# A graph network, expert mixture and attention kernel: four tables of node sums instead of two, and a sort that is numbered inside the edge stage

## The reference

```python
e = _mlp2(edge_feat, We1, be1, We2, be2)              # relu(e @ We1 + be1) @ We2 + be2
msg = jax.nn.relu(node_feat[src] + e)                 # 40000 x 256
out_h = jax.ops.segment_sum(msg, dst, num_segments=N_NODES)
out = _mlp2((1.0 + eps[0]) * node_feat + out_h, Wn1, bn1, Wn2, bn2)
```

## Time and profile before

| what | value |
|---|---|
| median of three runs | 2723.11 us (2719.55 to 2726.37) |
| the profiled execution, its time on the device | 2718.02 us |
| its span in the profile | 2716.3 us |
| granted TensorE clock, mean over the span | 0.867 of full speed |
| busy: PE, DVE, POOL, ACT | 2088.1, 1647.1, 1394.8, 1007.2 us |
| costliest group: POOL L632, additions to the tables | 316, 551.3 us |
| POOL L623, gathers of node rows | 316, 327.3 us |

### The profile page before, as it was taken

The page is one execution under the profiler, slowest core; times in us unless marked ns, Lnnn a source line. Parts: engine busy times, 40 slices in busy tenths (PEclk is TensorE's granted clock), DMA queues, the critical chain, the costliest instruction groups (busy, mean ns, idle before and its releaser), DMA issues. The chain is left out here.

```text
span 2716.3 us, 46328 instructions
## 1 busy us (share of the span) xinstructions
PE 2088.1 (77%) x13095; PEld 1804.4 (66%) x13096; DVE 1647.1 (61%) x4774; ACT 1007.2 (37%) x1931; POOL 1394.8 (51%) x1131
## 2 busy tenths in 40 slices
PE   2599999999999999955629999990466666662778
PEld 2588888888888888855628888880444444441776
DVE  5477786666666666648464444445655555557774
ACT  1254445545445554432205555550222222221321
POOL 1387887877777877760001111105377777771000
PEclk9799999999999999977759999995777767765888
DMA  6466656666666666642116777762233333342001
GB/s 165 134 131 131 133 120 130 134 132 135 135 128 125 133 130 133 129 86 70 39 41 229 244 243 242 239 220 81 76 92 93 90 89 91 90 84 28 22 10 38
DMA packets 185998, 325.71 MB, mean 120 GB/s; under 512 B 27528, under 2 KB 109037, under 8 KB 185192
## 3 DMA queue, kind: packets, MB, share of 16 engines
q0 software_dynamic: 82080, 141.73, 25.8%
q1 hardware_dynamic: 102962, 181.83, 21.8%
q10 hardware_dynamic: 900, 1.50, 0.2%
HBM read 260.65 MB, written 64.30 MB: 120 GB/s over the span
## 5 line engine op out<-in xcount | busy, mean ns | idle before, releaser
L632 POOL DMA_INDIRECT edge_sums<-edge_agg,edge_slot x316 | 551.3, 1745 | 172.5 <-issue 78.8
L1750 POOL DMA_INDIRECT att_got<-head_table,att_idx x352 | 401.8, 1141 | 125.1 <-issue 107.0
L623 POOL DMA_INDIRECT edge_nf<-node_table,edge_node_idx x316 | 327.3, 1036 | 152.0 <-issue 89.0
L751 ACT ACTIVATE edge_whole<-edge_h_ps,edge_b 128x512 f32<-128x512 f32 x316 | 215.8, 683 | 482.2 <-PE edge_h_ps L468 478.4
L466 PE MATMUL edge_e_ps<-edge_w_high,edge_hid_low 128*128 128x256 f32 x1264 | 357.3, 283 | 0.1
L467 PE MATMUL edge_e_ps<-edge_w_low,edge_hid_high 128*128 128x256 f32 x1264 | 356.9, 282 | 0.0
L468 PE MATMUL edge_e_ps<-edge_w_high,edge_hid_high 128*128 128x256 f32 x1264 | 356.2, 282 | 0.0
L1780 PE MATMUL att_s_ps<-att_w,att_hot 128*125 128x258 f32 x704 | 277.0, 562 | 3.2 <-issue 1.8
L466 PE MATMUL edge_h_ps<-edge_eat_high,edge_w_low 128*128 128x512 f32 x632 | 248.9, 394 | 23.6 <-DVE edge_eat_low L811 23.6
L1361 POOL DMA_INDIRECT moe_rows<-node_table,moe_idx x54 | 51.9, 961 | 396.8 <-DVE moe_idx L1473 396.4
L825 DVE TENSOR_TENSOR edge_pre<-edge_e_ps,edge_nf 128x1024 f32<-128x1024 f32 x79 | 96.8, 1225 | 256.2 <-DMA edge_nf<-node_table,edge_node_idx 208.9
(11 more groups left out here) (344 smaller groups left out, 4424.4 us busy)
## 6 DMA issues: line engine op xcount, KB each, us to landing
moe_w<-in_L_ffn_w_dram SPq DMA_DIRECT2D x162, 512.0 KB, 4.7
edge_ea<-in_edge_attr_dram SPq DMA_DIRECT2D x77, 448.0 KB, 5.1
edge_dst_row<-dst_rows SPq DMA_DIRECT2D x79, 256.0 KB, 4.5
routed<-moe_out SPq DMA_DIRECT2D x54, 128.0 KB, 6.3
att_got<-head_table,att_idx POOLq DMA_INDIRECT x352, 2.8
edge_nf<-node_table,edge_node_idx POOLq DMA_INDIRECT x316
edge_sums<-edge_agg,edge_slot POOLq DMA_INDIRECT x316, 4.8
edge_ea<-in_edge_attr_dram SPq DMA_DIRECT2D x77, 64.0 KB, 5.3
```

Of the source, the lines that this page charges most:

```text
L623: pool.indirect_dma_start(nf[u][:, j, :], None, m.node_table[:, :], bass.IndirectOffsetOnAxis(ap=node_idx[u][:, j:j + 1], axis=0)).then_in ...
L632: pool.indirect_dma_start(m.sums[k][:, :], bass.IndirectOffsetOnAxis(ap=slot[u][:, j:j + 1], axis=0), agg[u][:, j, :], None, compute_op=AL ...
L751: act.activation(whole[c][:], h_ps[:, c % 2, 0:N], ACT.Relu, bias=b1[:, c:c + 1]).then_inc(hid_whole, 1)
L1750: pool.indirect_dma_start(got[v][:, j, :], None, m.head_table[:, :], bass.IndirectOffsetOnAxis(ap=idx[v][:, j:j + 1], axis=0)).then_inc(la ...
```

## The change

- `SUMS` becomes 4: each block of a group has its own table. POOL's additions to a table wait for those of the group before, `g * 16`. The tables that begin as zeros are three, and their DMAs (L606) stand right behind the weights, as soon as x has landed.
- PE's turn becomes `hidden(g)`, transposes, `edges_out(g)`, `gather_same(g-1)`.
- ACT makes all four high parts of the hidden layer, and the message's high part after them; DVE makes none. DVE's `one_group` begins with hidden low parts 0 and 1; then come `add_nodes`, low parts 2 and 3 and `message_low`.
- The sort is numbered in the edge stage: after group 23 PE computes the totals into the PSUM of the hidden layer, DVE takes the offsets and then numbers one bucket after each of groups 24 to 43 (`number_bucket`). The node stage no longer has `number`.
- The node stage loads four tables into SBUF, two of them in the space of `y` and `spare`; the weights go through ACT's queue. For each step POOL adds the tables 2 and 3, DVE 0 and 1, and then both.

The core of the diff:

```diff
-SUMS = 2
+SUMS = 4
@@ def edge_messages: SP
+                sp.wait_ge(zeros_ready, 1)
+                sp.wait_ge(m.x_landed, 32)
+                for k in range(1, SUMS):
+                    sp.dma_start(m.sums[k][0:N_NODES, :].rearrange("(p t) d -> p t d", t=TILES),
+                                 zeros[0:LANES, :].unsqueeze(1).to_broadcast([LANES, TILES, DIM])).then_inc(sums_begun, 16)
                 sp.wait_ge(rows_made, 1)
...
-                sp.wait_ge(zeros_ready, 1)
                 for k in range(SUMS):
                     sp.dma_start(m.sums[k][N_NODES:N_NODES + P, :], zeros[:]).then_inc(sums_begun, 16)
-                for k in range(1, SUMS):
-                    sp.dma_start(m.sums[k][0:N_NODES, :].rearrange("(p t) d -> p t d", t=TILES),
-                                 zeros[0:LANES, :].unsqueeze(1).to_broadcast([LANES, TILES, DIM])).then_inc(sums_begun, 16)
@@ POOL
-                def add_sums(g, u, n, first=False):
-                    for k in range(SUMS):
-                        j = n * SUMS + k
-                        if not (first and n == 0):
-                            pool.wait_ge(sum_landed[k], g * (16 * G // SUMS) + 16 * n)
+                def add_sums(g, u, tables, first=False):
+                    for k in tables:
+                        if not first:
+                            pool.wait_ge(sum_landed[k], g * 16)
...
@@ PE
-                    for u in range(2):
-                        hidden(g + u)
...
-                        transposes(1 - u, g * 16 + (32 + 32 * u))
-                        gather_same(g + (u - 1), 1 - u)
-                        edges_out(g + u)
+                        for u in range(2):
+                            hidden(g + u)
...
+                            transposes(1 - u, g * 16 + (32 + 32 * u))
+                            edges_out(g + u)
+                            gather_same(g + (u - 1), 1 - u)
...
+                turns(2, numbered)
+                pe.wait_ge(hid_whole, numbered * KH)
+                by_src.order.totals(pe, h_ps)
+                pe.wait_ge(by_src.order.offsets_ready, 1)
+                turns(numbered, tail)
@@ ACT
                 for c in range(KH):
                     hidden_relu(g, c)
-                    if c == 1 and first != 1:
-                        message_high(g - 1)
-                    if c % 2 == 0:
-                        even_high(g, c)
+                    hidden_high(g, c)
+                if first != 1:
+                    message_high(g - 1)
@@ DVE
+                for g in range(2 + TILES, numbered):
+                    one_group(g, g % 2)
+                by_src.order.offsets(dve, h_ps)
+                for g in range(numbered, numbered + TILES):
+                    one_group(g, g % 2)
+                    by_src.order.number_bucket(dve, g - numbered)
+                by_src.order.write_out(dve)
@@ class BucketSort
+    def number_bucket(self, dve, b):
...
+        one = slot[:] if b == 0 else self.part_i[:].bitcast(F32)
...
+        chain.link(nc.vector.scalar_tensor_tensor(one, self.seen[:, b, :], self.off[:, b:b + 1], self.mask[:, b, :], ALU.add, ALU.mult))
+        if b == 0:
+            chain.link(nc.vector.tensor_scalar(tile_f[:], units, last, None, ALU.is_ge))
+        else:
+            nc.vector.tensor_tensor(slot[:], slot[:], one, ALU.add)
+            chain.link(nc.vector.scalar_tensor_tensor(tile_f[:], units, last, tile_f[:], ALU.is_ge, ALU.add))
@@ def node_mlp
-        sums = [sb(f"sums{k}", [LANES, TILES, DIM]) for k in range(SUMS)]
+        sums = [m.y, m.spare] + [sb(f"sums{k}", [LANES, TILES, DIM]) for k in range(2, SUMS)]
...
+            @block.gpsimd
...
+                def add_late(n, u):
+                    nc.gpsimd.tensor_tensor(sums[2][:, tiles, :], sums[2][:, tiles, :], sums[3][:, tiles, :], ALU.add).then_inc(late_added, 1)
...
-                    nc.vector.tensor_tensor(z[u][:], sums[0][:, tiles, :], sums[1][:, tiles, :], ALU.add).then_inc(z_ready, 1)
+                    nc.vector.tensor_tensor(sums[0][:, tiles, :], sums[0][:, tiles, :], sums[1][:, tiles, :], ALU.add).then_inc(early_added, 1)
+                    dve.wait_ge(early_added, n + 1)
+                    dve.wait_ge(late_added, n + 1)
+                    nc.vector.tensor_tensor(z[u][:], sums[0][:, tiles, :], sums[2][:, tiles, :], ALU.add).then_inc(z_ready, 1)
...
-                by_src.order.number(dve)
```

More of the change, by code:

```diff
@@ L238, in __init__ @@
         self.tile_f = sb("tile_f", [1, self.units])
[L239 to L243, removed]
         if self.by_bucket:
-            self.numbers = ctx.enter_context(self.nc.sbuf_tensor(self.name + "_numbers", [LANES, self.buckets // 2, self.cols], F32))
-            self.part = ctx.enter_context(self.nc.sbuf_tensor(self.name + "_part", [LANES, self.cols], F32))
+            self.offsets_ready = sem(name + "_offsets_ready")
+        else:
+            self.sums = ctx.enter_context(nc.psum_tensor(name + "_sums", [P, 2, 512], F32))
     def count(self, dve):
@@ L275, in number @@
[L275 to L278, removed]
+        nc.tensor.matmul(sums[0:LANES, 0, 0:buckets], m.before[0:LANES, 0:LANES], self.mine[:], start=True, stop=True)
@@ new lines, in number @@
+    def number(self, dve):
+        nc, chain, units, buckets = self.nc, self.m.steps, self.units, self.buckets
+        mask, seen, last, off, slot = self.mask, self.seen, self.last, self.off, self.slot
+        self.offsets(dve, self.sums)
+        for b in range(buckets):
+            last_slots = nc.vector.scalar_tensor_tensor(seen[:, b, :], seen[:, b, :], off[:, b:b + 1], mask[:, b, :], ALU.add, ALU.mult)
+        chain.link(last_slots)
+        chain.link(nc.vector.tensor_reduce(slot[:], seen.rearrange("p b c -> p c b"), AX_X, ALU.add))
+        chain.link(nc.vector.tensor_tensor(
+            self.past, self.m.count[0:1, 0:units].unsqueeze(2).to_broadcast([1, units, buckets]),
+            last[0:1, :].unsqueeze(1).to_broadcast([1, units, buckets]), ALU.is_ge))
+        chain.link(nc.vector.tensor_reduce(self.tile_f[:], self.past, AX_X, ALU.add))
+        self.write_out(dve)
@@ L305, in number, with write_out @@
+    def write_out(self, dve):
+        nc, chain, out, slot, slot_i, part_i = self.nc, self.m.steps, self.out, self.slot, self.slot_i, self.part_i
         chain.link(nc.vector.tensor_copy(slot_i[:], slot[:]))
@@ L325, in _ @@
             def _(pe):
-                order.totals(pe)
+                order.totals(pe, order.sums)
             @block.vector
@@ L515, in edge_messages @@
     tail = (groups - 3) // 2 * 2
-    assert late % 2 == 0 and late <= tail
+    numbered = 2 + TILES + 2
+    assert late % 2 == 0 and late <= tail and SUMS == G
     with ExitStack() as ctx:
@@ L1043, in two @@
             return [sb(f"{n}{u}", shape, dt) for u in range(2)]
-        by_src.order.work(ctx)
         w1 = sb("w1", [P, KD, HID])
```

102 lines of the change are left out of this document (48 added, 54 removed).

## The result

The changed kernel takes 2778.1 us (2776.5 to 2785.8, 4 runs), the kernel before 2722.4 beside it: ratio 1.0209, 95% interval [1.0186, 1.0232], 56 us slower. The forecast was 2707 (2680 to 2738). The profiled spans are 2777.2 and 2716.3 us, 60.9 apart.

A forecast was written before the change was run, and what follows sets the result against it. POOL, never resting at 14.08 us a group, was taken to bound the loop. Terms: -47 (loop) + 8 + 3 (sort) + 15 (start) + 3.5 (node stage) + 1.5 (tail) = -16 us, giving 2707 us, range 2680 to 2738.

The forecast's parts named there:

- The loop: Edge loop: a group falls from 14.06 to 13.45 us, saving 47 us over 77 groups.
- A third loop binds these: Edge loop: later agg delays POOL's additions and so find_slots; with little room for gathers, 0.25 us a group added.
- POOL's own need: Edge loop: POOL needs 14.08 - 0.84 = 13.24 us a group without table waits, taken as 13.1.
- PE's own need: Edge loop: PE alone needs 12.88 us a group plus 0.3 for its new order, 13.2.
- The slot wait: Rival, edge loop: waits for slots replace table waits, T = 13.8 us a group, 2734 us in all; chance 0.22.
- The zeros are nearly free: Rival, start: SP queues all three tables and goes on, +3 instead of +15 us, 2695 in all; chance 0.15.
- the loads run faster: Rival, node stage: 11.3 MB at 300 GB/s take 38 us, 8 less, 2699 in all; chance 0.13.
- The sort: Edge loop: counting and numbering buckets cost 8 us, PE's stop at group 24 another 3 us.
- The start: Start: SP hangs behind three writes of zeros, node table leaves near 87.5 instead of 48.16 us; +15 us.
- The node stage: Node stage: numbering goes, but loads take 45.6 us, combine(2) is 4 us late and added sums cost 1.5; +3.5 us.

The follow-up runs named there:

- Gathers first: Changed kernel with POOL issuing all four gathers for group g+2 before it waits for agg(g), then the four additions: 2704.2 us, ratio 0.9932.
- the old turns: Changed kernel with the turns of PE, ACT and DVE as before, four tables and the sort in the loop kept: 2726.6 us, ratio 1.0012.
- fastest kernel: Changed kernel with POOL's four gathers ahead of its wait for agg and each table of zeros written by two DMAs: 2666.6 us, ratio 0.9825.
- the four buffers: Changed kernel with four slot buffers instead of two, written without waiting for the additions of the group before: 2761.6 us, ratio 1.0151.
- the edit to 112 + 13 partitions: Changed kernel with each table of zeros written by two DMAs, of 112 and 13 partitions, instead of one of 125: 2742.8 us, ratio 1.0079.
- the kernel with DVE's additions: Changed kernel with the node stage's sum of table 2 and table 3 on DVE instead of POOL: 2777.9 us, ratio 1.0227.
- the new turns alone: Kernel before with only the new turns of PE, ACT and DVE; two tables, zeros and sort as before: 2739.5 us, ratio 1.0049.

## Why the prediction was wrong

**The loop is the step that failed**, in the part "A third loop binds these". It gave 13.45 us a group, with 0.25 for a late landing of the additions and for the gathers, "landed about 4 us into the turn whose `add_nodes` comes at 5". The groups measured 14.39 us before the sort's part and 14.26 behind it, and the loop as a whole came out 69 us longer than forecast (+32.7 against -47 + 11), of the 77 us by which the profiled execution missed its 2702. The engines and the order of the loop were right, its closing was not: it was followed to `find_slots` and to the next low part, and the gathers were taken to have a microsecond to spare, when `add_nodes` waits for them in 44 of 61 groups. The lap above goes through the gathers and not through the slots: `agg`, 13.3 us of POOL's eight DMAs, a landing of 4.7, `add_nodes`, `edges_out`, `agg`, 28.6 for two groups, or 14.3 a group. With the new turns `agg` stands 6 us later, behind `edges_out`, and the gathers, though they do not need `agg`, stand behind it on POOL. Gathers first takes them out of the lap and gives 1.0 us a group back (0.2 of it by shorter issues); the old turns take `edges_out` out of it and give 0.7 back.

**POOL's own need was a term mis-sized.** "14.08 - 0.84 = 13.24", then 13.1, subtracted whole waits. But 0.30 us pass before every indirect DMA, a wait's row holds that gap too, and it stays when the wait goes. In the traces POOL needs its busy time plus 8 x 0.30: before 11.1 + 2.4 = 13.5, fastest kernel 11.0 + 2.4 = 13.4. With four tables and the gathers between the additions it is 13.6 to 13.7 (busy 11.24 in the old turns, 11.27 in the changed kernel). So even with waits at zero and no lap the forecast of 13.45 could not have been met. In the old turns four tables, with the sort in the loop, bring 14.05 to 13.77, a quarter of a microsecond; the full 0.84 was never there. The Trainium skill (Perfetto Trace Analysis, Identifying the Most-Contended Engine) judges GpSimd by its occupancy; here that was 79% for an engine that had nothing to give but 0.6 us a group, so the gaps belong to the sum.

**PE's own need was mis-sized too**, at 12.88 + 0.3 = 13.2. Before, 42 of the 76 groups take 12.88 us; with the new turns none takes less than 13.40. PE waits for the low parts of the hidden layer, as the forecast said, but for 0.26 us a group in the gathers-first kernel; the other quarter of a microsecond is not accounted for.

**The rivals.** "The slot wait" had the right sign (2734, T = 13.8), and DVE's waits for slots did grow to 244 us. Yet its mechanism carries 16 us of time, as the four buffers show, the largest part around groups 22 to 24. "The zeros are nearly free" and "the loads run faster" are refuted, by +17.9 us at the start and by the 49.8 us of the loads.

**The sort** was put at 8 + 3 us, and groups 22 to 44 took 14.91 us against 14.39 ahead of them, 11 us in all. That the sums agree is luck. The 19 groups 25 to 43, each with a bucket numbered behind it, took 14.32 us, those behind group 44 took 14.26: the numbering cost 1 us, and counting (14.39 in groups 2 to 22) under 3, against 4 each. Groups 23 and 24, at the totals and offsets, took 18.7 and 15.5, together 5.6 more than two groups of 14.3, against the forecast's 3. And group 22 took 21.8, for a reason that is not the sort's: it holds DVE's addition of `bn2` to x, which the kernel before has as well (14.9 us there), behind a slot wait of 5.1 us, and with POOL held by it:
```profile
419.42 0.16 DVE L864 TENSOR_TENSOR edge_slot<-edge_moves,edge_dst 128x4 int32<-128x4 f32 x1 [5.13 <-DMA edge_sums<-edge_agg,edge_slot]
...
420.79 5.48 DVE L934 TENSOR_TENSOR x<-x,row_a 125x5120 f32<-125x5120 f32 x1
...
421.72 5.44 POOL L632 DMA_INDIRECT edge_nf<-node_table,edge_node_idx  x1 [0.31 <-issue]
```
In the gathers-first kernel groups 22 to 24 take 17.8, 14.8 and 13.5 us, and those that number take 13.40 like all others. Nor is the sort what made the kernel slower: with it in the old turns the mean group is 13.77.

**The start** came as argued: SP hung for three writes at 0.34 of the DMA engines, 121 GB/s, the node table left at 85.04 (87.5 forecast), +17.9 against +15. The Trainium skill (DMA: Bandwidth & Descriptors, Why a DMA increments its semaphore by 16 and not by 1) has the outer size decide how many engines a DMA uses. With the forecast only the window stood for it; the edit to 112 + 13 partitions is the test, and the 70 us of hung issues before the node table became 36.

**The node stage** was +10.2 against +3.5. The order of events was right (weights, then a wait for the second part of the tables). Two terms were short: the loads took 49.8 us and not 45.6, as the 11.3 MB came at 227 GB/s and not at 247, and the stage behind them ran 1.9 us longer, not 0.5 shorter. Of that at most 1.2 us can be POOL's additions, by the kernel with DVE's additions, whose node stage is no shorter as a whole.

What stays open: the new turns cost 14 us with two tables and 52 with four. Part of it is that four tables gain 21 us in the old turns (14.05 to 13.77 a group, with the sort in the loop) and 4.5 at most in the new, where the lap of 14.3 binds either way. The other 20 us or so are not accounted for, and no profile of the new turns alone near its median is there to place them. The two comparisons also differ in the sort, which stands in the loop in both kernels of the 52 us and in neither of the 14.

## What to carry to other kernels

An engine whose busy time and ordinary gaps fill the window is full, whatever its busy share says; of a wait that will go, subtract only what exceeds the gap. When a wait on one queue goes, look for the loop through the instructions that stand behind another wait on that queue without needing it: moving the gathers ahead of it turned a change that lost 2.1% into one that gains 0.7. The two need each other: without the early gathers four tables gained next to nothing in the loop of the new turns, and with two tables the early gathers brought the mean group from 14.54 only to 14.32, with four from 14.48 to 13.48. And a copy is priced by how its outer size divides over the DMA engines before it is multiplied by three.

## What the runs showed of the hardware

- DVE and POOL slow each other on additions with both inputs in SBUF: on POOL one of 125x512 took 1.26 us alone and 1.70 to 1.74 beside DVE's, and DVE's took 1.78 and 1.64 beside POOL's, 0.69 alone. The Trainium skill (SBUF — State Buffer, Who interferes with whom) says that a DVE instruction with two SBUF inputs contends with GpSimd's reads; the numbers agree. Moving POOL's additions to DVE made the program no shorter.
- A long addition on DVE with both inputs in SBUF holds the issue of an indirect DMA on POOL. In the trace of each of the 14 kernels (before, after and the twelve) one indirect DMA begins during DVE's 5.48 us addition of `bn2` (125x5120) and keeps POOL busy for 4.75 to 5.98 us, ending 0.8 to 1.5 us behind the addition; the usual gather takes 1.0 and the usual addition to a table 1.6 to 1.8.
- Gathers issued four in a row take 0.99 us each, between additions 1.08 (500 to 1100 us, 178 and 168 of them).
- A table of 2.56 MB written from 125 partitions hung SP for 21 to 26 us (DMA share 0.34); as 112 + 13 partitions three of them and a small store took 36 (16.97 to 53.14), over 200 GB/s.
